# Convolution taps of two tiles issued alternately on VectorE, and a reduction moved ahead of a PSUM read, in a one-core language-model tower

## The reference, cut to what matters

```
h   = quantised_table[x]                        # row scale = max|row| / 127, then round and clip
z, xBC, dt = layernorm(h) @ in_proj_w.T         # xBC has 640 channels
xconv[t] = conv_b + sum_{k<4} conv_w[:, k] * xBC[t - 3 + k]   # depthwise, per channel, zero before t = 0
xBC = silu(xconv);  x, B, C = split(xBC)
y   = ssd(x * dt, dt * A, B, C) + D * x         # state space product, one chunk of 128 per sequence
h   = h + out_proj(rmsnorm(y * silu(z))) * gate + layernorm(h)
h   = h + expert mixture of layernorm(h)        # two routers of four experts, a capacity on the first
```

## Time and profile before

| | us |
|---|---|
| median of 3 runs | 1077.2 |
| lowest, highest | 1069.45, 1078.46 |
| the profiled execution | 1081.81 |
| its span in the trace | 1080.0 |
| VectorE busy in it | 648.5 |
| TensorE busy in it | 936.5 |
| mean granted TensorE clock | 0.928 of full |

### The profile page before, as it was taken

One profiled execution on the slowest core, in us unless ns is written; L12 is line 12 of the kernel. 1 busy time (PEld: TensorE's weight loads), 2 busy tenths in 40 slices (PEclk: granted clock), 3 DMA queues, 4 the chain that ended last, 5 costly groups with the idle time before them and its releaser, 6 DMA issues.

```text
span 1080.0 us, 18795 instructions
## 1 busy us (share of the span) xinstructions
PE 936.5 (87%) x5730; PEld 624.0 (58%) x5731; DVE 648.5 (60%) x2080; ACT 570.5 (53%) x1165; POOL 552.5 (51%) x735
## 2 busy tenths in 40 slices
PE   2688999999998999989999788989798787979995
PEld 2233555544554555545556666768576565858774
DVE  3678999899797998888895236777121111112211
ACT  2677888777776797777862422323223222323230
POOL 6234545557366564663524463334565656664543
PEclk9898999999899999998997769999798988989987
DMA  4910011101010101100101121235221211122211
GB/s 98 325 44 16 11 35 46 46 16 44 32 47 18 44 32 45 47 17 30 33 30 61 50 78 45 80 100 150 68 72 47 57 53 47 51 52 77 68 50 28
DMA packets 50178, 61.90 MB, mean 57 GB/s; under 512 B 22668, under 2 KB 41832, under 8 KB 49556
## 3 DMA queue, kind: packets, MB, share of 16 engines
q0 software_dynamic: 16704, 30.54, 10.1%
q1 hardware_dynamic: 28724, 24.91, 7.7%
q10 hardware_dynamic: 4640, 5.13, 1.6%
HBM read 36.22 MB, written 25.92 MB: 58 GB/s over the span
## 4 chain that ended last, share of the span: by engine, by line
PE 48%; DVE 24%; issue 11%; another core or an unknown queue 5%; ACT 5%; POOL 2%; DMA 2%; DVEq 1%; POOLq 0%; ACTq 0%
DVE xbc L1569 7%; PE cx L1320 6%; PE yb L1320 5%; PE mm L1165 5%; PE mm L1298 4%; PE mm L1291 4%; PE mm L1169 3%; PE sg L1291 3%; PE tp L1132 3%; PE misc L1180 3%; PE sg L1083 3%; PE yb L1114 2%; DVE mix L1590 2%; DVE ybuf L1603 2%
## 5 line engine op out<-in xcount | busy, mean ns | idle before, releaser
L1569 DVE SCALAR_TENSOR_TENSOR xbc<-mm,cw,xbc 128x508 f32<-128x508 f32 (+2 forms) x231 | 167.2, 735 | 26.6 <-ACT xbc L819 22.1
L997 ACT ACTIVATE ht<-mm,b1s 128x256 f32<-128x256 f32 x102 | 44.7, 472 | 250.1 <-PE sg L1291 126.3
L701 POOL DMA_INDIRECT out_dram<-osb,ids_s x80 | 81.9, 1024 | 139.2 <-DVE osb L1998 124.3
L1165 PE MATMUL mm<-xt_a,win_a 128*128 128x512 f32 x248 | 139.7, 656 | 11.3 <-DVE xbc L1569 10.7
L1998 DVE TENSOR_TENSOR osb<-cx,res 128x192 f32<-128x192 f32 x40 | 14.3, 356 | 193.4 <-remote 110.4
L558 POOL TENSOR_TENSOR ybuf<-ybuf,zs 128x384 f32<-128x384 f32 x64 | 64.9, 1015 | 116.1 <-DVE ybuf L1603 114.2
L682 POOL DMA_INDIRECT xg<-hr_dram,ids x80 | 79.3, 992 | 46.2 <-issue 24.3
L1291 PE MATMUL mm<-fx_a,w1a_t 128*128 128x256 f32 x240 | 81.6, 423 | 20.8 <-issue 20.7
L1320 PE MATMUL cx<-w2s,ht 128*128 x408 | 81.5, 349 | 14.1 <-issue 14.1
L1320 PE MATMUL yb<-w2s,ht 128*128 x408 | 80.4, 348 | 3.7 <-issue 3.6
L804 ACT ACTIVATE dec<-sg 128x384 f32<-128x384 f32 x128 | 55.8, 488 | 49.3 <-PE sg L1083 43.3
(11 more groups left out here) (305 smaller groups left out, 2107.2 us busy)
## 6 DMA issues: line engine op xcount, KB each, us to landing
hr_dram<-hr SPq DMA_DIRECT2D x16, 768.0 KB
w2s<-in_w2c_dram SPq DMA_DIRECT2D x4, 576.0 KB
w2s_u<-in_w2u_dram ACTq DMA_DIRECT2D x4, 576.0 KB
list_c<-fill SPq DMA_DIRECT2D x2, 1032.0 KB, 12.2
list_u<-fill SPq DMA_DIRECT2D x2, 1032.0 KB, 18.2
w1a<-in_w1c_dram SPq DMA_DIRECT2D x4, 384.0 KB
w1a_u<-in_w1u_dram ACTq DMA_DIRECT2D x4, 384.0 KB
xg<-hr_dram,ids POOLq DMA_INDIRECT x80
```

The costliest lines, as they stand in the source:

```text
L701: nc.gpsimd.indirect_dma_start(out=out_rows, out_offset=bass.IndirectOffsetOnAxis(ap=ids_s[:, v, t, 0:1], axis=0), in_=osb[:, v, t, :], in ...
L1165: mmul(tile_bank(g2, m)[:, :], win_a[:, column(m):column(m) + P], xt_a[:, p, :], start=True, stop=False)
L1569: ins = stt(out=dst_[:, :, back:L], in0=src[:, :, 0:L - back], scalar=cw[:, m, TAPS - 1 - back:TAPS - back], in1=dst_[:, :, back:L], op0=A ...
```

## The change

Tiles 0 and 1, and tiles 2 and 3, are no longer convolved one after the other. `conv_pair(m)` issues the first tap of tile m, the first of tile m + 1, the second of m, the second of m + 1, and so on. Each tap of a tile still waits for the tap before it of that tile. The first tap of tile m + 1 waits for ScalarE's `start(m + 1)`. Tile 4 is as before. `quantise` of the next group moves from behind `weights(2)` to ahead of `side_read`. The other engines' streams are unchanged.

```
+                def conv_pair(m):
+                    if g2 is None:
+                        return
+                    p, link = g2 % 2, chains["tap"]
+                    first = link.n
+                    for back in range(1, TAPS):
+                        for k in range(2):
+                            if back == 1:
+                                dve.wait_ge(s_ci, XT * g2 + m + k + 1)
+                            else:
+                                link.join(first + 2 * (back - 2) + k + 1)
+                            src = tile_bank(g2, m + k)[:, :].rearrange("p (j t) -> p j t", j=GS)
+                            dst_ = xbc[:, p, m + k, :].rearrange("p (j t) -> p j t", j=GS)
+                            ins = stt(out=dst_[:, :, back:L], in0=src[:, :, 0:L - back],
+                                      scalar=cw[:, m + k, TAPS - 1 - back:TAPS - back], in1=dst_[:, :, back:L],
+                                      op0=ALU.mult, op1=ALU.add)
+                            if back < TAPS - 1:
+                                link.go(ins)
+                            else:
+                                ins.then_inc(s_cv, 1)
...
                 weights(0)
-                conv(0)
-                conv(1)
+                conv_pair(0)
                 logits()
                 weights(1)
                 y(0)
                 places()
-                conv(2)
-                conv(3)
+                conv_pair(2)
+                if t + 1 < NG:
+                    quantise(t + 1)
                 side_read()
                 steps_abs()
                 weights(2)
-                if t + 1 < NG:
-                    quantise(t + 1)
                 y(1)
                 conv(4, (soft_sum, soft_inverse))
```

## The result

The changed kernel takes 1101.16 us (median of 4 runs, 1098.36 to 1102.47) against 1077.83 (4 runs, 1069.45 to 1081.52): **1.0214 times as long, 95% interval 1.0178 to 1.0250**, 23 us more. The forecast was 1092 with a range of 1076 to 1104: slower, as forecast, and inside the range, but by half as much again as the sum had it.

What follows compares the result with a forecast made beforehand. Each turn was taken as one loop through VectorE, TensorE and ScalarE, with the handover from the taps to project(3) on it. Delays of 17.0 us less 2.0 for `side` gave +15, median 1077.2 to 1092, range 1076 to 1104.

Steps and rivals of the forecast that it cites:

- The pair's own gain: On VectorE, alternated taps start 0.66 us apart; six taps take 4.05 us instead of 4.50, saving 0.45 a pair.
- The handover: From VectorE's taps to TensorE's project(2) and project(3): project(3) 1.5 us later in even turns, 10.5 us over seven.
- Turn 4 from pair to pair: Sign: turn 4 lasts 33.6 us from pair to pair where it is 32.15.
- The clock: Rival: TensorE idles longer ahead of `side`, the granted clock falls in five turns, 12 us more, 1104; chance 0.12.
- The deduction for `side`: TensorE's stretched `side` loses less from a later start: 0.4 us in each of five even turns, 2.0 us off.
- Turn 2: Turns 2, 3, 9, 15: chain leaves taps earlier or runs through the second pair; 0.8 us each, 3.2 in all.
- The move of `quantise`: On VectorE ahead of `side_read`: 1.5 us later in turn 1, behind the gather; worth nothing on the chain elsewhere.
- VectorE's own time as the bound: Rival: with 2.0 us of slack at TensorE's project(2), each pair's gain shortens the loop, -13.5 us, 1064; chance 0.10.
- Slack in TensorE: Rival: the stretch of `side` swallows the delay in every middle turn, +6 us, 1083; chance 0.23.
- The signs named in advance: Second tap idle 0.9 us, project(2) idle about 2.4, pairs 5.0 and 4.05 us long, turn 1's L920 after 48.5.

Runs made afterwards that it cites:

- e6: Kernel before, one number changed on TensorE so that project(2) also waits for tile 1: 1041.30 us against 1000.78, ratio 1.0401.
- e10: Kernel before with only tiles 0 and 1 interleaved, tile 0's last tap fourth: 1079.46 us against 1076.99, ratio 1.0008.
- e5: Whole change plus two unused matmuls on TensorE ahead of project(2), against the kernel before: 1019.58 us against 1000.78, ratio 1.0185.
- e1: Both pairs alternated, quantise left in place, against the kernel before: 1037.58 us against 1000.58, ratio 1.0378.
- e4: Kernel before with only tiles 2 and 3 alternated, quantise left in place: 1003.88 us against 1000.58, ratio 1.0045.
- e9: Both pairs, quantise in place, start(1) ahead of decays(1), cbx(1) ahead of project(2), against the kernel before: 1076.87 us against 1076.99, ratio 1.0000.
- r1: Whole change compared a second time with the kernel before: 1108.07 us against 1076.99, ratio 1.0273.
- e7: Whole change with ScalarE's start(1) moved ahead of decays(1), against the kernel before: 1025.69 us against 1000.78, ratio 1.0246.
- r2: Kernel before, unchanged, run again for its trace: 1078.75 us in one profiled run, against 1076.99.
- e8: Kernel before with only quantise moved, in turns 2 to 14 and not in turn 1: 1003.78 us against 1000.78, ratio 1.0025.

## Why the prediction was right, and where its sum was not

The time came out slower, inside the range, and the place of the loss was named in advance. That the number fell inside the range is in part luck: two terms of opposite sign were wrong, the second comparison's +31 us is more than the range's upper end allowed (+27), and so is the +37 of the pairs alone on the chips of 1000 us.

- **The pair's own gain**: six taps in 4.01 us, forecast 4.05. Taps of different tiles start (4.01 - 0.75) / 5 = 0.65 us apart, those of one tile 0.77. The Trainium skill (page "VectorE: DVE Perf Modes", section "The DRAIN you can't avoid") has it that the next op does not start until the pipe has emptied, and adds that an op that is not held starts earlier. By the first alone the pair would not have become shorter; the trace's 0.65 us goes with the second.
- **The handover** (the 1.5 us a turn): right in place and nearly in size. `project(3)` is 1.33 us later in turn 4; the 1.67 us of work that the forecast put between the two products is 1.51 when nothing is waited for. e6 shows that TensorE's wait alone makes a loss of this size, e10 that the first 0.7 us of lateness are free, and e5, with the clock kept up, leaves 18.8 us for waits and turn 1 where the sum had 17.0.
- **Turn 4 from pair to pair**: 170.44 - 137.42 = 33.02 us, forecast 33.6, before 32.15. The missing 0.6 us: 0.17 is the handover's, and most of the rest is a stretch of `side` that I had taken for absent in this turn. The chain of before has 0.52 us of "issue" inside `side`, from 135.61 us on, and in the changed kernel its rows follow each other without a gap.
- **The clock** is the step that failed. It stood as a rival with 0.12, in five turns, and apart from the forecast. It fell in nearly every turn, and it is no other way for the kernel to go but a second consequence of the same waits: with them filled (e5) it falls in 4 places and not in 14. On the chips of 1000 us it is about 18 us of 37, or more, by e5 against e1. On those of 1077 us it was not taken away; there the trace shows 15 us more for the same products, of which an unknown part lies on the path.
- **The deduction for `side`**: 2.0 us was far too small on the chips of 1077 us. Its stretch nearly vanished, some 13 us of TensorE's time in the stretch of 84 to 530 us. Clock and stretch have opposite signs, so the sum of +15 came near to the measured +23 with two of its terms wrong.
- **Turn 2** (0.8 us in the sum): the starts of L832 put turn 2 at +5.4 us. Two waits meet there, tile 0's for `project(2)` and tile 2's for `project(4)`, each with a fall of the clock behind it. The wait of `project(4)` was not in the sum at all: the forecast had followed the second pair to VectorE's next wait, and not to TensorE, which reads tile 2. e4 prices the second pair at 2 to 7 us.
- **The move of `quantise`**: turn 1 right for tile 4 (forecast at 49.9, seen at 49.92), but the turn's end moved by 2.2 us instead of 1.5, since `rounded` on ScalarE, which the forecast did not follow, moved by 2.24. For the rest 0 was forecast and 0 to 5 measured.
- **The rivals**: VectorE's own time as the bound: against it stands e9, where the pair of turn 4 is 0.5 us shorter, TensorE waits 0.27 us for it, and the kernel's time is equal. Slack in TensorE is half true on the chips of 1077 us: it is what the vanished stretch gave back. The signs named in advance were there: the second tap's 0.88 us, the 2.39 us before `project(2)`, the pairs of 4.97 and 4.01 us, L920 at 48.99.

What stays open: why `side` is stretched on some chips and not on others, and why a later `side` escapes it (the trace names no releaser for those idle times); and what beside the wait decides the clock. It stays up in turn 4 of the changed kernel after 2.39 us and falls in the same turn of r1 after the same 2.39; in turn 9 of the changed kernel the product takes 2.07 us behind a wait of only 0.58, and in e7 some take up to 2 us after waits of 1.04. So the length of the wait alone does not tell. The whole change on a chip of 1000 us stays unmeasured, and e9 and e10 were not run on one.

## What to carry to other kernels

When two equal chains are interleaved on one engine, the first one's result comes later: look at who waits for it, and how much other work its reader could do first. Up to that slack it is free, and reordering the reader (here `cbx(1)`, together with `start(1)`) is what made it so. Look at every reader of both chains: here the first tile of the second pair had one too. When a wait on TensorE grows, read the granted clock and the duration of the first matmul behind it, not only the wait: the price can double (37 us against 19 here), and it belongs in the sum rather than among the rivals.

## What was not expected of the hardware

- A wait of TensorE's product between two full stretches of work lowered the granted clock to 0.5, the 1.2 GHz level, in about every turn: 1.49 us idle in turn 5, 2.39 in turn 4 of r1, 0.58 in turn 9, with products of 2.07 or 2.08 us behind it instead of 1.12. In e10, where `project(2)` waits up to 1.09 us, it took 1.12 or 1.13 us behind each of those waits.
- Matmuls whose results nobody reads, on the engine that bounds the turns, made the kernel 18 us faster (e5 against e1).
- The same kernel takes 1077 us on some chips and 1001 on others, 76 us apart; by r2 against e8 most of it, 62 us, lies in the expert tiles.
